# The second feed-forward stage: the gate product's maximum taken inside the product and from the integers

## The reference

```python
def act_qdq(x):
    scale = jnp.maximum(jnp.max(jnp.abs(x)) / qmax, 1e-12)      # qmax = 32767
    return jnp.clip(jnp.round(x / scale), -qmax - 1.0, qmax) * scale

def fixed_qdq_u16(x):
    scale = 1.0 / 65536.0
    return jnp.clip(jnp.round(x / scale), 0.0, 65535.0) * scale

x = act_qdq(x)
up = act_qdq(x @ lpbq_dequant(w_up).T)
gate = act_qdq(x @ lpbq_dequant(w_gate).T)
sig = fixed_qdq_u16(jax.nn.sigmoid(gate))
gate = act_qdq(gate * sig)
o = act_qdq(gate * up)
return o @ lpbq_dequant(w_down).T
```

## Time and profile before

| | |
|---|---|
| median of the runs | 1180.78 us (1177.42 to 1181.47) |
| the profiled execution | 1173.82 us, of it the span 1172.1 us |
| mean granted TensorE clock | 0.956 |
| PE busy | 1082.8 us (92% of the span) |
| VectorE (DVE) busy | 951.2 us (81%) |
| ScalarE (ACT) busy | 603.2 us (51%) |
| GpSimd (POOL) busy | 471.3 us (40%) |

### The profile page before, as it was taken

The page is one execution under the profiler, slowest core; times in us unless marked ns, Lnnn a source line. Parts: engine busy times, 40 slices in busy tenths (PEclk is TensorE's granted clock), DMA queues, the critical chain, the costliest instruction groups (busy, mean ns, idle before and its releaser), DMA issues.

```text
span 1172.1 us, 19846 instructions
## 1 busy us (share of the span) xinstructions
PE 1082.8 (92%) x6208; PEld 893.9 (76%) x6208; DVE 951.2 (81%) x2564; ACT 603.2 (51%) x1339; POOL 471.3 (40%) x543
## 2 busy tenths in 40 slices
PE   7899999998799988995999999999999879999997
PEld 5677787886587755442998999989999768887886
DVE  4788998886676799798668888988888659888886
ACT  1666767774455889577882333433333323333332
POOL 1235455342000578664002444545555343434333
PEclk7999999999799999787999999999999979999999
DMA  9000000000233586698305011101000000000000
GB/s 277 6 1 2 1 2 1 1 2 12 87 128 144 179 278 239 227 362 296 91 2 166 3 45 46 46 1 46 1 1 1 1 1 19 18 18 27 18 18 28
DMA packets 50626, 83.25 MB, mean 71 GB/s; under 512 B 4700, under 2 KB 36272, under 8 KB 50544
## 3 DMA queue, kind: packets, MB, share of 16 engines
q1 hardware_dynamic: 49167, 81.43, 20.5%
q10 hardware_dynamic: 1376, 0.79, 0.3%
HBM read 45.98 MB, written 36.23 MB: 70 GB/s over the span
## 4 chain that ended last, share of the span: by engine, by line
PE 40%; DVE 6%; issue 3%; ACT 2%; POOL 1%; DVEq 0%; ACTq 0%; POOLq 0%
PE m_ps L2327 13%; PE a_ps L1261 11%; PE a_ps L1209 5%; PE f_ps L2228 5%; PE a_ps L1224 3%; DVE a_U L1387 1%; PE m_ps L2355 1%; DVE a_xnl L1354 1%; ACT a_xnT L1287 1%; PE m_ps L2375 1%; DVE m_xl L2525 0%; ACT f_oq L2210 0%; DVE a_mx L1379 0%; PE m_ps L2364 0%; PE a_ps L1513 0%
## 5 line engine op out<-in xcount | busy, mean ns | idle before, releaser
L1261 PE MATMUL a_ps<-VW,a_PT 128*128 128x256 f32 x640 | 144.0, 380 | 0.0
L1261 PEld LDWEIGHTS a_ps<-VW,a_PT 128*128 128x128 f32 x640 | 120.3, 190 | 15.2
L1319 POOL TENSOR_TENSOR a_xrs<-a_xve,mhalf 128x1 f32<-128x1 f32 x32 | 18.8, 586 | 200.2 <-DVE a_xve L1436 200.2
L1301 ACT ACTIVATE a_U<-a_U 128x1280 f32<-128x1280 f32 x32 | 40.7, 1271 | 108.9 <-DVE a_U L1387 108.9
L2432 POOL TENSOR_TENSOR m_half<-m_half 128x512 f32<-128x512 f32 x32 | 41.0, 1282 | 128.0 <-ACT m_half L2392 128.0
L1280 ACT COPY a_PT<-a_ps 128x512 f32<-128x512 f32 (+1 forms) x96 | 46.1, 518 | 79.9 <-PE a_ps L1224 79.9
L2327 PE MATMUL m_ps<-m_wh,m_xh 128*128 128x512 f32 x256 | 86.2, 418 | 0.0
L1034 DVE TENSOR_SCALAR a_U<-a_ps 128x320 f32<-128x320 f32 x128 | 59.2, 484 | 30.4 <-PE a_ps L842 21.4
L2076 POOL TENSOR_SCALAR f_sg<-f_sg 128x1024 f32<-128x1024 f32 x24 | 37.6, 1566 | 108.5 <-ACT f_sg L1971 108.1
L1326 POOL TENSOR_TENSOR a_U<-a_U,a_rc 128x1280 f32<-128x1280 f32 x32 | 74.6, 2333 | 15.8 <-DVE a_rc L1366 15.8
L2327 PE MATMUL m_ps<-m_wh,m_xl 128*128 128x512 f32 x256 | 80.4, 395 | 0.0
(11 more groups left out here) (257 smaller groups left out, 3156.3 us busy)
## 6 DMA issues: line engine op xcount, KB each, us to landing
up_scratch<-f_ub SPq DMA_DIRECT2D x24, 512.0 KB, 3.0
f_ul<-up_scratch SPq DMA_DIRECT2D x24, 512.0 KB, 5.4
key_scratch<-p_keys SPq DMA_DIRECT2D x8, 640.0 KB, 6.5
vw_scratch<-p_vw SPq DMA_DIRECT2D x16, 320.0 KB, 5.7
k_raw<-key_scratch SPq DMA_DIRECT2D x8, 640.0 KB, 5.9
VW<-vw_scratch SPq DMA_DIRECT2D x4, 1280.0 KB, 5.8
xs<-in_x SPq DMA_DIRECT2D x4, 1024.0 KB, 12.3
h_scratch<-f_hh SPq DMA_DIRECT2D x8, 512.0 KB, 2.6
```

What stands on the lines that cost most here:

```text
L1261: last = pe.matmul(Y[:, 0:D], PTs[t.p][:, j, :], fold.values[t.batch % 2][:, j, :], start=(j == 0), stop=(j == NJ - 1))
```

## The change

The largest absolute value of the product is the larger of its maximum and of minus its minimum. The changed kernel finds the two sides apart:

- VectorE's product becomes `tensor_tensor_reduce`: it writes minus the product (scale -1) and the maximum of what it writes, starting from 0, into a column of `am2`. That is the negative side. The reduction at line 2116 is gone.
- For the positive side a running maximum `run` (128x512, int16) is kept over the gate's integers: two `tensor_tensor` maxima of 512 columns for each unit, the second waiting for the first. Since sigmoid grows with its argument, the largest product belongs to the largest integer. At the end `run` is reduced to one value per row; ScalarE takes its sigmoid, VectorE clips and rounds it, multiplies it by the integer and takes the larger of it and the negative side.
- GpSimd's two instructions are recast: add GRID and take the smaller with TOP, then take the larger with GRID and subtract GRID. The product needs no subtraction then.
- VectorE's order in a unit is: two maxima, maximum of the up values, product. Before, it was product, maximum of the up values, maximum of the product.
- VectorE's loop over the tiles is written out in full.
- The next part reads the negated product with a negated scale, `nksl`, one more link behind `integer_scale`; `SCALED` counts it.

The diff, cut to its core:

```diff
+    TOP = GRID + (U16S - 1) / U16S
...
-    SCALED = 16
+    SCALED = 17
...
+        run = nc.alloc_sbuf_tensor_at("f_run", [P, CW], I16, offset=hold + 43008 - 2 * P * 4)
...
                 for k in range(KT):
                     act.wait_ge(p1.s_T, k + 1)
                     p1.query_out(act, 0, k)
+                act.wait_ge(s_rp, 1)
+                act.activation(big[:, 1:2], big[:, 0:1], ACT.Sigmoid, scale=sga).then_inc(s_rs, 1)
                 act.wait_ge(s_g2, NU)
...
-                    act.activation(gq[u % 2][:], unit(u), ACT.Copy, scale=ksl).then_inc(s_g3, 1)
+                    act.activation(gq[u % 2][:], unit(u), ACT.Copy, scale=nksl).then_inc(s_g3, 1)
...
-                        pool.tensor_scalar(v, v, (U16S - 1) / U16S, 0.0, ALU.min, ALU.max).then_inc(s_cap, 1)
+                        pool.tensor_scalar(v, v, GRID, TOP, ALU.add, ALU.min).then_inc(s_cap, 1)
                         pool.wait_ge(s_cap, t.of(lambda n: UC * n + q + 1))
 
-                        pool.tensor_scalar(v, v, 1.0, GRID, ALU.mult, ALU.add).then_inc(s_su, 1)
+                        pool.tensor_scalar(v, v, GRID, GRID, ALU.max, ALU.subtract).then_inc(s_su, 1)
...
-                        dve.wait_ge(s_su, t.of(lambda n: UC * n + q + 1))
-                        dve.scalar_tensor_tensor(unit(t.n * UC + q), sg[par][:], GRID, iq[q][:], ALU.subtract,
-                                                 ALU.mult).then_inc(s_g2, 1)
+                        dve.wait_ge(s_gq, t.of(lambda n: UC * n + q + 1))
+                        for e in range(2):
+                            v = iq[q][:, e * CW:(e + 1) * CW]
+                            if t.t0 == 0 and q == 0 and e == 0:
+                                dve.tensor_copy(run[:], v).then_inc(s_run, 1)
+                            else:
+                                dve.wait_ge(s_run, t.of(lambda n: 2 * (UC * n + q) + e))
+                                dve.tensor_tensor(run[:], run[:], v, ALU.max).then_inc(s_run, 1)
+                        if t.t0 == NCH - 1 and q == UC - 1:
+                            dve.wait_ge(s_run, 2 * NU)
+                            dve.tensor_reduce(big[:, 0:1], run[:], AX.X, ALU.max).then_inc(s_rp, 1)
                         dve.wait_ge(s_ue, t.of(lambda n: MF * n + 2 * q + 2))
                         dve.tensor_reduce(amu[:, bass.ds(t.n * UC + q, 1)], ub[par][:], AX.X, ALU.max,
                                           apply_absolute_value=True).then_inc(s_ua, 1)
-                        dve.wait_ge(s_g2, t.of(lambda n: UC * n + q + 1))
-                        dve.tensor_reduce(am2[:, bass.ds(t.n * UC + q, 1)], unit(t.n * UC + q), AX.X, ALU.max,
-                                          apply_absolute_value=True).then_inc(s_am2, 1)
+                        dve.wait_ge(s_su, t.of(lambda n: UC * n + q + 1))
+                        dve.tensor_tensor_reduce(unit(t.n * UC + q), sg[par][:], iq[q][:], -1.0, 0.0, ALU.mult,
+                                                 ALU.max, am2[:, bass.ds(t.n * UC + q, 1)]).then_inc(s_g2, 1)
                         if t.t0 == NCH - 1 and q == 1:
                             p1.mask_key(dve, 0)
-                pipeline(dve, body, 0, NCH - 1, 2, 5)
+                for t in range(NCH):
+                    body(At(t))
...
+                dve.wait_ge(s_rs, 1)
+                dve.tensor_scalar(big[:, 2:3], big[:, 1:2], GRID, TOP, ALU.add, ALU.min).then_inc(s_rq, 1)
+                dve.wait_ge(s_rq, 1)
+                dve.tensor_scalar(big[:, 2:3], big[:, 2:3], GRID, GRID, ALU.max, ALU.subtract).then_inc(s_rq, 1)
+                dve.wait_ge(s_g2, NU)
+                dve.tensor_reduce(big[:, 3:4], am2[:], AX.X, ALU.max).then_inc(s_rq, 1)
+                dve.wait_ge(s_rq, 3)
+                dve.scalar_tensor_tensor(loc[:, 3:4], big[:, 2:3], big[:, 0:1], big[:, 3:4], ALU.mult,
+                                         ALU.max).then_inc(s_loc, 1)
...
+                link(dve, dve.tensor_scalar(nksl, ksl, -1.0, None, ALU.mult))
```

More of the change, by code:

```diff
@@ L1647, in ffn @@
     s_hs, s_b = [s("hs0"), s("hs1")], [s("b0"), s("b1")]
+    s_run, s_rp, s_rs, s_rq = s("run"), s("rp"), s("rs"), s("rq")
     s_um, s_ue, s_ua, s_uw = s("um"), s("ue"), s("ua"), [s("uw0"), s("uw1")]
-    s_gq, s_sg, s_cap, s_su, s_g2, s_am2 = s("gq"), s("sg"), s("cap"), s("su"), s("g2"), s("am2")
+    s_gq, s_sg, s_cap, s_su, s_g2 = s("gq"), s("sg"), s("cap"), s("su"), s("g2")
     s_ul, s_uq, s_g3, s_pr, s_am3 = [s(f"ul{i}") for i in range(4)], s("uq"), s("g3"), s("pr"), s("am3")
@@ L1662, in ffn @@
         amu = sbuf(st, "amu", [P, NU])
+        big = sbuf(st, "big", [P, 4])
         am2 = sbuf(st, "am2", [P, NU])
@@ L1668, in ffn @@
         (sh, ih, sup, kup, sga, kga, ssl, ksl, spr, kpr, tmp, sps) = [sc[:, i:i + 1] for i in range(12)]
+        nksl = sc[:, 13:14]
         hold = nc.sbuf_base
@@ L2091, in _ @@
                 p1.null_key(pool, 1)
-                pool.wait_ge(s_sc, SCALED - 4)
+                pool.wait_ge(s_sc, SCALED - 5)
                 rounded(0)
@@ L2124, in _ @@
                 dve.tensor_reduce(loc[:, 2:3], amu[:], AX.X, ALU.max).then_inc(s_loc, 1)
-                dve.wait_ge(s_am2, NU)
-                dve.tensor_reduce(loc[:, 3:4], am2[:], AX.X, ALU.max).then_inc(s_loc, 1)
+                dve.wait_ge(s_rs, 1)
[7 more added lines that the diff above has]
+                                         ALU.max).then_inc(s_loc, 1)
                 fold_max(dve, 2)
```

## The result

The changed kernel took 1262.38 us in the median (1260.99 to 1263.55, four runs), the kernel before beside it 1181.12 (1177.42 to 1183.6). The ratio is 1.0708, with an interval of 1.0676 to 1.0740: 81 us slower by the medians, some 84 by the ratio. The forecast was 1194.0 us with a range of 1182 to 1213, so the sign held and the size was missed by far.

What follows compares the result with a forecast made beforehand. Stage end hangs on VectorE and the nearly equal ScalarE-to-PE chain; 4.1 us per unit moves mask_key from 469.85 to 482.8, with the 0.25 link +13.2 us: 1187.0 profiled, plus 7 for timed runs, 1194.0 us, range 1182 to 1213.

Steps and rivals of the forecast that it cites:

- part 5: GpSimd's two tensor_scalars in the second feed-forward stage: only their operations change, existing forms take 1.04 and 1.05 us; adds nothing.
- Parts 1 and 2: VectorE per unit: maximum of the product removed, 1.13 us; product with a maximum costs today's 1.13 plus 0.05 for the accumulator.
- The rival of half pace: VectorE's product with a maximum runs at half pace: another 1.07 us, 5.2 per unit, +35 us; chance 0.08.
- Part 3: Two int16 maxima of 128x512 on VectorE: 0.80 us per unit by the lower bound taken, 1.34 by the upper.
- The rival of one element per cycle: VectorE's int16 maxima pass one element per cycle, each holding GpSimd out 0.57 us: +23 us, range +20 to +28; chance 0.18.
- Part 4 and the order written out: VectorE's own work 3.1 us per unit; taking turns with GpSimd at SBUF makes 4.1 us per unit, against 3.39.
- The marks: Signs expected in the profile after: GpSimd means 1.6 or more without idle time, maxima 0.42 us alone, products 3.8 to 4.4 apart.
- The rival of maxima that fit in the gaps: VectorE's int16 maxima fit between GpSimd's instructions, no slowdown: below 3.45 us per unit only 0.25 us is left; chance 0.17.
- Part 6: Tiny ScalarE and VectorE instructions at the stage's end: some 1.5 us within 4.1 of room, nothing; negated scale's link +0.25 us.
- Part 7: VectorE's hardware loop unrolled: register instructions go, more code comes, starts stay 1.13 us apart; nothing.
- A faster VectorE could win at most 0.3 us here.: End of the second feed-forward stage: mask_key(0) at 469.85 us also waits for ScalarE to PE, free at 469.57.
- the mechanism that the forecast argued for: VectorE instructions with two SBUF tensors and GpSimd tensor_scalars exclude each other: exclusive time rises from 2.87 to 3.47 us per unit.

Runs made afterwards that it cites:

- the first program: Separate program, no network computed: GpSimd tensor_scalar pairs and VectorE instructions timed alone and beside each other; min/max and mult/add 1.04 us, the two new pairs 3.63.
- the kernel with cheap pairs: Changed kernel with GpSimd's two instructions as mult/add pairs (plus 128, minus 128), clip at 65535/65536 left out: 1196.46 us, ratio 1.0136 against before.

## Why the forecast missed

**The step that failed is part 5**, "GpSimd's two tensor_scalars only change their operations: nothing". It was an extrapolation from two rows, min/max at 1.04 and mult/add at 1.05 us, to "the operations don't matter". The rows were right and the inference was not: the first program shows that both belong to the few fast pairs, and that nearly every other pair tried takes 3.63. In place of nothing the term was 2 x (3.64 - 1.04) = 5.2 us of GpSimd's time per unit, and as it made GpSimd the bound, 7.32 - 3.39 = 3.93 us per unit of the stage's. Alone, with nothing of the rest of the change, the two pairs measured a ratio of 1.0756. The working could have seen the gap: it bounded the unseen int16 maximum from both sides and didn't do so for two pairs of operations that no row showed. No rival had it, so the range could not hold it either.

**The other steps**, as the kernel with cheap pairs shows them:

- *Parts 1 and 2.* The product with a maximum takes 1.23 us alone. Its value is read out in a record of its own of 0.08 us, but the next instruction starts beside it: product to next start is 1.14 us where it was 1.13. 0.05 had been taken. The rival of half pace is false. The Trainium skill, "Vector Engine (DVE) Microarchitecture Reference", section "Points that are easy to get wrong", which the forecast named there, has such an instruction at half its throughput. This case's traces don't agree: 1.23 us with the accumulator and 1.23 without it, for 1024 elements of fp32 and int16. The trace records the new product as a custom instruction and the plain one as SCALAR_TENSOR_TENSOR; the latter with an accumulator was not run.
- *Part 3.* The int16 maximum takes 0.42 us for 512, the lower bound; the same maximum on fp32 took 0.69 in the same program. The rival of one element per cycle is false. The row of bf16 tensor_tensor in the Trainium skill, "VectorE: DVE Perf Modes", section "The perf-mode tier table (the rule you actually need)", fits int16 too, by this number.
- *Part 4 and the order written out.* 4.1 us per unit forecast, 4.108 measured; product(1) at 394.4 forecast, 394.75 measured; mask_key(0) at 482.8 forecast, 484.72 measured; +13.2 us forecast, +16 (10 to 22) measured, +14.8 between the two profiled executions. The way from product(21) to mask_key(0), 6.4 us in the sum, took 7.6 (it also takes off 0.12 us of slack where it had named 0.28). VectorE's waiting came out right in sum, 2.06 us in two units. Its pattern did not: the distances swing between some 4.2 and 3.9, not 4.75 and 3.35. The two distances that the prediction does write out, 5.49 and 3.40, have a mean of 4.45; how they settle at 4.05 is not shown there. So that 4.1 and 4.108 lie so close is in part luck.
- *The marks.* There were int16 maxima of 0.42 us alone and over 1 us when held out, products 3.9 to 4.3 us apart (but for one of 4.64 at the start), ScalarE waiting for products, and a granted clock of 0.91 in the stage (383 to 486 us) where it was 0.93. Two marks failed. GpSimd's tensor_scalars had means of 1.16 and 1.45 us, not 1.6 or more in both lines. And GpSimd was idle for 33 us of the stage, where the forecast wanted no idle time, though its own order had GpSimd waiting for the sigmoid. The engine without idle time was VectorE.
- *The rival of maxima that fit in the gaps* is false: leaving them out gave the 16 us back.
- *Part 6* held in the kernel with cheap pairs: from mask_key(0) to the rows' maxima it took 10.01 us, as before. In the changed kernel it took 1.1 more, by a step that part 6 didn't name, GpSimd's null_key (L755) behind its own last tensor_scalar. The added link cost 0.20 us (PE's rows' maxima to ScalarE's first integers: 3.35 in place of 3.15), forecast 0.25. *Part 7*: nothing of it is to be seen; the kernel with the maxima left out is unrolled too and loses nothing.
- *"A faster VectorE could win at most 0.3 us here."* The kernel with cheap pairs and no maxima agrees: ratio 0.9996 with VectorE at 2.3 us of work per unit, and ScalarE's last copies no earlier in its trace. The interval alone would allow a gain of up to 4.4 us. The one with the rounding on VectorE (0.9999, at 2.9 us of work) is no clean test, as its stage is longer in the trace.

In the changed kernel the mechanism that the forecast argued for is hidden: "GpSimd's tensor_scalars lengthened" came true with a mean of 3.64, for another reason. In the listing the mark that separates the two is the duration's constancy. Contention gives 1.04, 1.9 and 2.2 in turn, as in the earlier trace rows; 24 times 3.637 is a price. And with VectorE idle for 78 us there is hardly anything to contend with.

## What to carry to other kernels

An instruction with another operation is another instruction: where no row has the new operation of an engine, its price is open and needs bounds and a rival like a new shape does, and above all on GpSimd. Measure it first; a program with each form twice costs one run. And an engine that looks fullest (VectorE, 3.39 us per unit) need not be worth relieving: here ScalarE stood 0.2 us behind it, and trading one instruction that excludes nobody for two that exclude GpSimd cost 16 us without the slow pairs.

## What the runs showed of the hardware that was not expected

- **GpSimd's tensor_scalar has three prices**, 128x1024 fp32 with constants: 1.04 us for min/max, mult/add, mult/mult and add/mult; 3.62 to 3.64 for every other pair of two operations tried; 2.77 for one operation alone. So a lone add (2.77) costs more than multiplying by 1 and adding (1.04). With scalars from SBUF (both of min/max, the multiplier of mult/add) these two were still fast, 1.18 and 1.11. Why these four pairs are cheap no run shows. The Trainium skill, "GPSIMD Engine Reference", section "4.1 Engine selection", calls elementwise work with one input roughly line-rate on this engine; the runs agree for the four fast pairs only.
- **A slow GpSimd instruction keeps VectorE's product out no longer than a fast one does.** The product got in 0.88 us after the start of a slow one of 3.64, and 0.89 after the start of a fast one of 1.04. What a slow one does in the rest of its time no run shows. The Trainium skill, "SBUF — State Buffer", section "Who interferes with whom", has the loser blocked for the winner's whole instruction; that fits the fast pairs here and not the slow ones.
- **VectorE's rounding pair add/subtract takes 0.69 us** for the same 128x1024 for which GpSimd, with add/subtract, takes 3.63.
